# Last stage of a fused transformer kernel: softmax sums from ScalarE's accumulator, sums spread over heads by small tiles, SiLU through tanh, maxima in three parts

## The chip, the cores and the metric

The kernel runs on one core of one Trainium2 chip. The metric is the device time of one execution in microseconds (us). A core has five engines with queues of their own, which run in the order of the program and wait for each other through semaphores: TensorE (PE; its weight loads are PEld), VectorE (DVE), ScalarE (ACT), GpSimd (POOL) and SyncE (SP).

## The reference

Eight sequences of 256 tokens, 512 wide, go through four blocks, each added to the residual `x` with a gate:

```
x = x + tanh(g_xattn[0]) * L0_xattn(layernorm(x), ctx)      # causal attention, 16 heads of 32
x = x + tanh(g_ffn[0])   * L0_ffn(layernorm(x))             # ternary weights, silu(gate) * up, rms_norm
x = x + tanh(g_xattn[1]) * L1_xattn(layernorm(x), ctx)      # below
x = x + tanh(g_ffn[1])   * L1_ffn(layernorm(x))             # below

# L1_xattn: q, k after rms_norm with a weight; 16 heads of 32; 256 keys; not causal
scores = q k^T / sqrt(32); probs = softmax(scores); out = (probs v) o_w^T + o_b

# L1_ffn: weights ternary with one scale, activations rounded to 8 bits per token
gv = bitlinear(rms(x) * w_norm, w_gv)                       # 256x512 @ 512x4096
value, gate = split(gv); u = value * silu(gate)
out = x + bitlinear(u, w_out)                               # 256x2048 @ 2048x512
```

The change touches only the last two blocks, which the kernel runs as one stage, called the last stage below.

## The kernel before

Everything stays on the chip: `X` holds the residual of all sequences, `W1` the ternary weights of the last block, `ARENA` all other tiles of SBUF (so that the profile calls nearly every tile ARENA or W), `bank` the eight PSUM banks of 128 x 512 f32. The last stage is a hand-written software pipeline in turns. In turn t (3 to 7, the full turns) it does, for the sequence f = t: projections of queries and keys and their norms; for b = t-1: scores, maxima, probabilities and the weighing of the values; for c = t-2: the output projection and the inputs of the feed-forward; for d = t-3: the feed-forward. A turn for b = 7 (called turn 8) and a closing part follow. The order in each engine's queue is written out by hand, and each engine waits on semaphores.

Per sequence b the attention has these steps. There are 16 heads, in four groups g of four (one head j on each 32 partitions and on each bank 0 to 3).

- `c_scores(b, g)`, four times, spread over the first part of the turn: TensorE writes the scores of four heads, tokens on partitions, into banks 0 to 3 (L745); VectorE takes the maximum of each row (L1625). The banks are then free for the next group.
- `c_max_parts`, `c_max_turn`, `c_max_rows`: the negated maxima are split into two bf16 parts (L1633, L1635), turned so that tokens lie along the free dimension (L754), and copied to `MT` (L1640).
- `c_probs(b, g)`, four times in the second part of the turn: TensorE computes the scores again, with keys on partitions (L764), adds the negated maxima by a matmul with a selection matrix `selc` (L768), and ScalarE takes exp (L1178).
- `c_weigh(b, g)`: TensorE multiplies the values by the probabilities, and a matrix of ones by the same probabilities, which gives the sums of the softmax, repeated over the 32 rows of a head (both L783). VectorE takes the reciprocal of the sums (L1656) and multiplies (L1658).

The feed-forward of d has eight pieces j in a turn: `d_value_gate(d, j)` on TensorE writes a gate into one bank and a value into another (L795, 4 + 4 matmuls); ScalarE makes `silu(scale * gate)` (L1195, called `d_gate`), which frees the gate's bank; VectorE multiplies by the scaled value (L1725), and after each odd piece takes a maximum for the rounding (L1731). `d_scale_u` (L1737 to L1741) makes the scale, `d_round_u` (L1207) and `d_integers16` (L1750) round, `d_turn_u` transposes (L425, copied at L1002), and `d_out_product` (L825) is the last matmul.

Silu and Exp lie in different activation tables. `warm(...)` (L1182) is placed in ScalarE's queue where the table changes, twice a full turn.

Banks 4 to 7 are shared by all these results. A list gives the order of the tenants of each bank, and a tenant may be written when the one before it has raised its semaphore:

```
places.turn(turn, ("g0 v1 g3 pq0 v6 v7 ut0.0 y0 xt0", "v0 po1 v3 g4 v5 g7 tq1 w1 w2 w3", "po0 g2 kt0 v4 pq1 w0 qt1 ut1.1 y1",
                   "g1 v2 kt1 g5 g6 mt tq0 ut0.1 qt0 ut1.0 xt1"))
```

Here `g`, `v` are gate and value of a piece, `w` the weighed values, `po`, `pq` projections, `kt`, `tq`, `xt`, `ut`, `qt`, `mt` transposes, `y` the result. TensorE's order in the first part of a full turn is: scores 0, piece 0, po0, piece 1, scores 1, po1, pieces 2 and 3, scores 2, kt, pq0, pieces 4 and 5, scores 3, pq1, piece 6, mt, piece 7, and then the second part begins with probs 0.

## Time and profile before

| | us |
|---|---|
| median of 3 runs | 1142.21 (1140.67 to 1143.71) |
| the profiled execution | 1139.14 |
| its span in the trace | 1137.4 |
| full turns 3 to 7 (722.53 to 1025.42) | 302.9 |
| turn 8, first part (1025.42 to 1057.50) | 32.1 |

The page of the profile gives the busy time of each engine and the groups of instructions by line. Times in the rows are us from the start of the span. A timeline row gives start, duration, engine, line, operation, output<-input, count, and in brackets how long the engine sat idle before it and who released it. Successive rows of one engine can overlap, since the engine starts one instruction while the one before still drains: what an instruction costs in a row of such is the distance of the starts. TensorE runs an f32 matmul as two instructions, so that eight f32 matmuls stand as x16.

### The profile page before, as it was taken

Reading aid. Unit: us, or ns where it says so; the run is one execution under the profiler, and the core shown is the slowest. Engines: PE = TensorE matmul, PEld = TensorE weight load, DVE = VectorE, ACT = ScalarE, POOL = GpSimd, SP = SyncE. Lnnn points to the kernel's source line nnn. Section 1 sums busy time; section 2 is a strip of 40 time slices with the busy share of each in tenths; the row PEclk is TensorE's granted clock in tenths of the full one; section 3 lists DMA queues with packets and bytes.
Section 4 is the critical chain, followed back from the end, with each engine's and each line's share of the span. In section 5 each row is a group of like instructions: output and inputs, shape, how many; then the busy total and the mean of one; then the engine's idle time right before and its main releaser. Section 6 shows DMA issues by size and latency. Waiting matters only on the chain.

```text
span 1137.4 us, 25529 instructions
## 1 busy us (share of the span) xinstructions
PE 1096.0 (96%) x10342; PEld 669.3 (59%) x10450; DVE 832.7 (73%) x1440; ACT 567.2 (50%) x918; POOL 74.5 (7%) x180
## 2 busy tenths in 40 slices
PE   8899999999999999999999999899999999999998
PEld 3455555556777777777777655455454545454543
DVE  5688888788767648566565667886868778777795
ACT  3676667766433333333333452455554637372654
POOL 0000000000000000000001012010101010101010
PEclk9899999999999999999999999999999999999999
DMA  9565555443212011021010201101010100000001
GB/s 361 185 194 169 181 193 156 154 122 122 67 38 65 20 38 37 20 75 28 29 57 20 84 2 38 37 2 56 1 57 1 57 1 30 10 11 11 10 10 38
DMA packets 29268, 79.24 MB, mean 70 GB/s; under 512 B 3041, under 2 KB 3297, under 8 KB 28897
## 3 DMA queue, kind: packets, MB, share of 16 engines
q1 hardware_dynamic: 29152, 77.61, 21.0%
q8 instruction: 84, 1.38, 0.5%
q14 instruction: 32, 0.25, 0.1%
HBM read 65.02 MB, written 12.58 MB: 68 GB/s over the span
## 4 chain that ended last, share of the span: by engine, by line
PE 89%; issue 3%; ACT 3%; DVE 2%; DMA 2%; SPq 1%; POOL 0%; ACTq 0%; DVEq 0%; POOLq 0%
PE bank L587 10%; PE bank L586 10%; PE bank L692 10%; PE bank L672 9%; PE bank L545 9%; PE bank L795 8%; PE bank L425 5%; PE bank L825 5%; PE bank L783 5%; PE bank L745 3%; PE bank L764 3%; PE bank L477 2%; PE bank L498 2%; PE bank L510 2%; PE bank L450 2%
## 5 line engine op out<-in xcount | busy, mean ns | idle before, releaser
L586 PE MATMUL bank<-ARENA,W 128*128 128x256 f16 x1024 | 227.3, 273 | 0.7 <-issue 0.7
L587 PE MATMUL bank<-ARENA,W 128*128 128x256 f16 x1024 | 227.2, 273 | 0.0
L1002 ACT ACTIVATE ARENA<-bank 128x512 f32<-128x512 f32 (+3 forms) x143 | 92.9, 687 | 81.3 <-PE bank L425 32.6
L545 PE MATMUL bank<-ARENA 128*128 128x512 f32 x256 | 119.4, 609 | 1.4 <-DMA ARENA<-in_wkv 1.4
L795 PE MATMUL bank<-W,ARENA 128*128 128x512 bf16 x493 | 116.6, 382 | 2.5 <-issue 0.7
L692 PE MATMUL bank<-ARENA 128*128 128x512 f32 x256 | 116.9, 600 | 0.0
L672 PE MATMUL bank<-W,ARENA 128*128 128x512 bf16 x472 | 114.6, 379 | 2.2 <-issue 0.2
L586 PEld LDWEIGHTS bank<-ARENA,W 128*128 128x128 bf16 x1024 | 100.0, 98 | 19.5 <-issue 1.3
L587 PEld LDWEIGHTS bank<-ARENA,W 128*128 128x128 bf16 x1024 | 100.1, 98 | 17.9
L1002 ACT ACTIVATE ARENA<-ARENA 128x512 f16<-128x512 f32 x64 | 40.3, 630 | 136.1 <-DVE ARENA L1585 129.6
L1585 DVE SCALAR_TENSOR_TENSOR ARENA<-bank,ARENA 128x512 f32<-128x512 f32 x64 | 48.0, 750 | 76.4 <-PE bank L587 73.5
L1195 ACT ACTIVATE ARENA<-bank,ARENA 128x512 f32<-128x512 f32 x64 | 43.7, 685 | 112.7 <-PE bank L795 105.5
L1999 POOL TENSOR_TENSOR ARENA<-ARENA 128x2 f32<-128x2 f32 (+1 forms) x72 | 49.2, 684 | 673.0 <-DVE ARENA L1372 435.4
L795 PEld LDWEIGHTS bank<-W,ARENA 128*128 128x128 bf16 x512 | 49.0, 98 | 66.3 <-issue 11.6
L1116 ACT ACTIVATE ARENA<-bank 128x512 f32<-128x512 f32 x64 | 38.2, 596 | 91.5 <-PE bank L587 91.4
L1382 DVE TENSOR_REDUCE ARENA<-bank 128x4 f32<-128x512 f32 x64 | 58.3, 952 | 34.6 <-PE bank L450 34.4
L1625 DVE TENSOR_REDUCE ARENA<-bank 128x4 f32<-128x1024 f32 x64 | 75.2, 1218 | 9.3 <-PE bank L745 9.3
L545 PEld LDWEIGHTS bank<-ARENA 128*128 128x128 f32 x256 | 47.4, 192 | 56.4 <-issue 52.5
L672 PEld LDWEIGHTS bank<-W,ARENA 128*128 128x128 f16 x512 | 49.9, 99 | 48.8 <-issue 1.9
L1591 DVE TENSOR_TENSOR ARENA<-ARENA 128x512 f16<-128x512 f32 x64 | 44.2, 691 | 46.5 <-ACT ARENA L1002 46.5
L1656 DVE RECIPROCAL ARENA<-bank 128x256 f32<-128x256 f32 x32 | 56.2, 1756 | 29.6 <-PE bank L783 29.6
L692 PEld LDWEIGHTS bank<-ARENA 128*128 128x128 f32 x256 | 46.6, 190 | 52.6 <-issue 51.5
(179 smaller groups left out, 1766.5 us busy)
## 6 DMA issues: line engine op xcount, KB each, us to landing
W<-in_w SPq DMA_DIRECT2D x48, 512.0 KB, 4.0
ARENA<-in_w SPq DMA_DIRECT2D x24, 512.0 KB, 3.6
kv_store<-ARENA SPq DMA_DIRECT2D x32, 256.0 KB, 3.8
W<-kv_store SPq DMA_DIRECT2D x15, 512.0 KB, 4.0
ARENA<-in_ctxT SPq DMA_DIRECT2D x8, 512.0 KB, 3.8
X<-in_x SPq DMA_DIRECT2D x8, 512.0 KB, 5.8
ARENA<-in_ctx SPq DMA_DIRECT2D x8, 512.0 KB, 5.9
out<-X SPq DMA_DIRECT2D x16, 256.0 KB, 2.0
```

What stands on the lines that cost most here:

```text
L425: mm = pe.transpose(to[:, k * P:(k + 1) * P], tile, one)
L545: mm = pe.matmul(bank, bufA["KT"][:, b % 2 * KD + k, t * P:(t + 1) * P], W[:, k, :], start=(k == 0), stop=(k == KD - 1 and what == 1))
L586: pe.matmul(bank[:, i * S:(i + 1) * S], W0[:, at:at + P], xt_half(b, 0)[:, k, :], start=(k == 0), stop=False)
L587: mm = pe.matmul(bank[:, i * S:(i + 1) * S], W0[:, at:at + P], xt_half(b, 1)[:, k, :], start=False, stop=(k == KD - 1))
L672: mm = pe.matmul(banks[6 + t], hx(q, what)[:, i * S + t * P:i * S + (t + 1) * P], W0[:, UP_AT + m * D:UP_AT + (m + 1) * D], start=(m == 0 ...
L692: pe.matmul(to, src[:, k, t * P:(t + 1) * P], WQ[w][:, k, :], start=(k == 0), stop=False)
L783: mm = pe.matmul(part(to, j)[:, what * S:(what + 1) * S], lhs, bufC["PT"][:, h % 8, kb * S:(kb + 1) * S], start=(kb == 0), stop=True, skip ...
L795: mm = pe.matmul(to, QQ[d][:, t, k * P:(k + 1) * P], W1[:, at:at + D], start=(k == 0), stop=(k == KD - 1))
L825: mm = pe.matmul(to, UT[d, t][:, k * P:(k + 1) * P], W1[:, UP_AT + k * D:UP_AT + (k + 1) * D], start=(k == 0), stop=(k == KH - 1))
L1002: return act.activation(to, src, ACT.Copy)
L1382: got = v.tensor_reduce(NM[:, t, :, g % 2], bank[:, 0:4, t * P:t * P + (t + 1) * P], AX_X, ALU.max, negate=True)
L1625: got = v.tensor_reduce(NM[:, t, :, g], bank[:, 0:4, t * S:(t + 1) * S], AX_X, ALU.max, negate=True)
```

## The change

- For the sequences b = 2 to 6 (`summed_apart`), the ones-matmuls of `c_weigh` go (8 f32 matmuls for each of the four groups), and so does VectorE's reciprocal of each group. Instead, ScalarE takes exp of the first scores in place in PSUM, with the negated maximum as bias, and its accumulator gives the row sums: `c_sums`, 32 activations of 128 x 256 per sequence. The next group of scores may be written only after these are done (`s.c_se`).
- VectorE inverts the 32 sums per token, splits them into three bf16 parts (`c_sum_parts`), TensorE turns them (`rt`, 2 transposes), VectorE copies them (`c_sum_rows`), TensorE spreads them over the rows of the heads by 16 matmuls of 32 x 32 tiles into two banks (`rb0`, `rb1`), ScalarE copies these into `OT` (`c_spread_sums`), and VectorE multiplies.
- For d = 0 to 5 (`by_tanh`), silu(z) is computed as z/2 * (1 + tanh(z/2)): ScalarE takes tanh, VectorE makes `(tanh + 1) * gate` in an operation of its own (`s.d_gg`, which now frees the gate's bank), and then multiplies by the value. Tanh and Exp need no change of table here, so that the `warm` calls of the full turns go.
- The negated maxima are split into three bf16 parts in place of two.
- The factor of the scores moves from ScalarE's exp into the query's scale.
- VectorE's and ScalarE's orders are rearranged: in the first part of a turn the sums stand between the gates in ScalarE's queue.

```diff
         for turn in range(3, NB):
-            places.turn(turn, ("g0 v1 g3 pq0 v6 v7 ut0.0 y0 xt0", "v0 po1 v3 g4 v5 g7 tq1 w1 w2 w3", "po0 g2 kt0 v4 pq1 w0 qt1 ut1.1 y1",
-                               "g1 v2 kt1 g5 g6 mt tq0 ut0.1 qt0 ut1.0 xt1"))
+            places.turn(turn, ("g0 v1 g3 pq0 v6 v7 rb0 ut0.0 y0 xt0", "v0 po1 v3 g4 v5 g7 tq1 w1 w2 w3", "po0 g2 kt0 v4 pq1 rt w0 qt1 ut1.1 y1",
+                               "g1 v2 kt1 g5 g6 mt tq0 rb1 ut0.1 qt0 ut1.0 xt1"))
...
@@ tensor_program: c_scores
                     for j in range(4):
+                        if summed_apart(b) and g:
+                            pe.wait_ge(s.c_se, 32 * (b - FIRST) + 8 * (g - 1) + 2 * (j + 1))
...
+            def c_turn_sums(b):
+                to, sem, value = bank_c("rt", b)
+                pe.wait_ge(sem, value)
+                pe.wait_ge(s.c_rhl, b - FIRST + 1)
+                for t in range(TB):
+                    mm = pe.transpose(as16(to, BF16)[:, t * P:(t + 1) * P], bufC["RHL"][:, t, :], keep["identb"])
+                mm.then_inc(s.c_rt, 1)
+
+            def c_spread_sums(b):
+                for k in range(2):
...
+                    pe.wait_ge(s.c_rtr, b - FIRST + 1)
+                    for n in range(2):
+                        for j in range(4):
+                            mm = pe.matmul(part(to, j)[:, n * S:(n + 1) * S], part(keep["selc"], j)[:, 2 * k + n, 0:DH], part(bufC["RT"], j),
+                                           start=(n == 0), stop=True, skip_group_check=True)
+                    mm.then_inc(s.c_rb, 1)
...
@@ c_weigh
-                for what in range(2):
+                for what in range(1 if summed_apart(b) else 2):
...
@@ turns, TensorE
                 c_turn_q(f)
+                c_turn_sums(b)
                 c_probs(b, 1)
+                c_spread_sums(b)
                 c_weigh(b, 0)
...
@@ scalar_program
+            def c_sums(b, g, banks_of=(0, 1, 2, 3)):
+                for j in banks_of:
+                    for t in range(TB):
+                        h, scores = NG * j + g, banks[j][:, t * S:(t + 1) * S]
+                        act.wait_ge(s.c_rhl, b - FIRST)
+                        act.wait_ge(s.c_scr, 4 * b + g + 1)
+                        act.activation(scores, scores, ACT.Exp, bias=bufC["NM"][:, t, h:h + 1], accum_out=bufC["sums"][:, t, h:h + 1]
+                                       ).then_inc(s.c_se, 1)
...
             for turn in range(3, NB):
                 d_gate(d, 0)
+                c_sums(b, 0)
                 d_gate(d, 1)
                 c_square_k(f, 0)
                 c_square_k(f, 1)
                 d_residual(d, 0)
+                c_sums(b, 1, (0, 1))
+                d_gate(d, 2)
+                c_sums(b, 1, (2, 3))
+                d_gate(d, 3)
                 d_residual(d, 1)
-                d_gate(d, 2)
-                d_gate(d, 3)
                 c_turn_k(f)
+                c_sums(b, 2, (0, 1))
                 c_square_q(f, 0)
                 d_gate(d, 4)
+                c_sums(b, 2, (2, 3))
+                d_gate(d, 5)
                 both(d_round_u, d, 0)
-                d_gate(d, 5)
+                c_sums(b, 3, (0, 1))
                 c_square_q(f, 1)
                 d_gate(d, 6)
+                c_sums(b, 3, (2, 3))
                 d_gate(d, 7)
-                warm(ACT.Exp)
                 c_probs(b, 0)
                 c_turn_q(f)
                 c_probs(b, 1)
+                c_spread_sums(b)
                 both(d_turn_u, d, 0)
...
-                warm(ACT.Silu)
...
@@ vector_program: c_weigh
+                if summed_apart(b):
+                    v.wait_ge(s.c_rbr, 2 * (b - FIRST) + g // 2 + 1)
+                    v.tensor_tensor(bufC["OT"][:, g, :], to[:, 0:S], bufC["OT"][:, g, :], ALU.mult).then_inc(s.c_pvr, 1)
...
@@ d_value_gate
+                if by_tanh(d):
+                    v.scalar_tensor_tensor(out=gated, in0=gated, scalar=1.0, in1=bank_c(f"g{j}", d)[0], op0=ALU.add, op1=ALU.mult).then_inc(s.d_gg, 1)
+                    v.wait_ge(s.d_gg, 8 * d + j + 1)
...
@@ turns, VectorE
                 d_scale_u(d, 0)
-                d_weighted(c)
                 c_scores(b, 2)
                 d_value_gate(d, 4)
+                c_norm_q(f, 0)
                 d_value_gate(d, 5)
-                c_norm_q(f, 0)
                 c_scores(b, 3)
                 c_max_parts(b)
                 d_value_gate(d, 6)
                 c_max_rows(b)
-                d_integers16(d, 0)
                 c_norm_q(f, 1)
                 d_value_gate(d, 7)
+                c_sum_parts(b)
                 d_scale_u(d, 1)
+                c_sum_rows(b)
+                d_integers16(d, 0)
+                d_weighted(c)
+                c_weigh(b, 0)
                 d_peak(c)
                 d_inputs(c)
-                c_weigh(b, 0)
+                c_weigh(b, 1)
                 if f + 1 < NB:
                     stats(f + 1, s.c_ve)
-                c_weigh(b, 1)
```

`c_sum_parts` is a reciprocal of 128 x 32 and four more operations of that size, one after the other; `c_sum_rows` is one copy of 128 x 256 bf16.

## Rows read from the trace of the kernel before

**Rows 1.** The page: busy time, share of the span, instructions.

```profile
PE 1096.0 (96%) x10342; PEld 669.3 (59%) x10450; DVE 832.7 (73%) x1440; ACT 567.2 (50%) x918; POOL 74.5 (7%) x180
```

**Rows 2.** The chain of work that ended last, inside one full turn, by line.

```profile
by line: PE bank L692 23.5%; PE bank L795 23.3%; PE bank L783 12.5%; PE bank L825 11.3%; PE bank L425 7.9%; PE bank L745 7.2%; PE bank L764 7.1%; ACT ARENA L1002 1.7%; ACT ARENA L1178 1.7%; PE bank L768 1.6%; PE bank L694 1.1%; issue 1.0%; 
```

**Rows 3.** Windows: full turns, one turn's two parts, turn 8's first part.

```profile
core 0: us, PE busy (x) PEld busy (x) DVE busy (x) ACT busy (x) POOL busy (x), PEclk, DMA share, GB/s
722.53:1025.42 302.89, 294.86 (x2400) 153.60 (x2422) 236.55 (x399) 162.86 (x240) 30.92 (x89) 1.00 0.08 25
844.27:878.80 34.53, 34.37 (x173) 16.14 (x175) 26.85 (x41) 12.65 (x22) 5.62 (x17) 1.00 0.09 29
878.80:904.57 25.77, 24.79 (x312) 14.77 (x313) 20.64 (x41) 20.02 (x27) 0.70 (x1) 1.00 0.10 26
1025.42:1057.50 32.08, 29.55 (x198) 14.43 (x204) 26.89 (x44) 11.44 (x16) 3.27 (x11) 1.00 0.03 9
```

**Rows 4.** Timeline of TensorE in that turn.

```profile
852.56 1.15 PE L745 MATMUL bank<-W 32*128 32x256 f32 x16
...
876.86 0.28 PE L754 MATMUL bank<-ARENA 128*128 128x128 bf16 x2
...
878.80 1.15 PE L764 MATMUL bank<-W 32*128 32x256 f32 x16
879.77 0.40 PE L768 MATMUL bank<-ARENA 32*128 32x256 bf16 x8
...
884.43 1.05 PE L783 MATMUL bank<-ARENA 128*32 128x256 f32 x16
885.41 1.07 PE L425 MATMUL bank<-ARENA 128*128 128x128 bf16 x16
```

**Rows 5.** Timeline of VectorE in the same full turn.

```profile
854.64 2.35 DVE L1625 TENSOR_REDUCE ARENA<-bank 128x4 f32<-128x1024 f32 x2
...
860.04 1.27 DVE L1678 BATCH_NORM_STATS2 ARENA<-X 128x6 f32<-128x512 f32 x2
...
861.51 0.72 DVE L1725 SCALAR_TENSOR_TENSOR W<-bank,ARENA 128x512 f32<-128x512 f32 x1
862.27 1.22 DVE L1731 TENSOR_REDUCE ARENA<-W 128x1 f32<-128x1024 f32 x1
...
864.68 1.40 DVE L1691 SCALAR_TENSOR_TENSOR ARENA<-X,ARENA 128x512 f32<-128x512 f32 x2
...
876.38 0.19 DVE L1635 TENSOR_TENSOR ARENA<-ARENA 128x32 bf16<-128x32 f32 x1
...
886.84 1.75 DVE L1656 RECIPROCAL ARENA<-bank 128x256 f32<-128x256 f32 x1
```

**Rows 6.** Timeline of ScalarE in that turn.

```profile
851.89 0.69 ACT L1195 ACTIVATE ARENA<-bank,ARENA 128x512 f32<-128x512 f32 x1 [4.69 <-PE bank L795]
...
862.76 1.09 ACT L1002 ACTIVATE W<-bank 128x512 f32<-128x512 f32 x2 [1.82 <-PE bank L425]
...
878.83 1.28 ACT L1182 ACT_TABLE_LOAD   x1
...
882.10 1.57 ACT L1170 ACTIVATE W<-bank,ARENA 128x256 f32<-128x256 f32 x4
```

**Rows 7.** Groups by line and form, last stage: busy us, mean ns of one.

```profile
L1170 ACT ACTIVATE W<-bank,ARENA 128x256 f32<-128x256 f32 x20 | 7.9, 490 | 0.0
```

**Rows 8.** Timeline of ScalarE in the first stage: accumulator, 256-wide copy.

```profile
227.22 1.08 ACT L1055 ACTIVATE W<-W 128x1024 f32<-128x1024 f32 x1
228.17 0.22 ACT L1055 ACTIVATION_READ_ACCUMULATOR W<-W 128x1 f32 x1
228.26 0.61 ACT L1002 ACTIVATE ARENA<-bank 128x512 f32<-128x512 f32 x1
...
232.11 0.38 ACT L1002 ACTIVATE W<-bank 128x256 f32<-128x256 f32 x1 [1.81 <-PE bank L510]
232.39 1.05 ACT L1012 ACTIVATE W<-W 128x1024 bf16<-128x1024 f32 x1
```

More of the change, by code:

```diff
@@ L168, in build @@
         keep, kept = views(ARENA, KEEP)
+        keep["abs_sum"], keep["scl"] = keep["spare"][:, 0:24], keep["spare"][:, 24:48]
         rest = ARENA[:, (kept + 31) // 32 * 8:]
@@ L762, in c_probs @@
                     for j in range(4):
+                        if summed_apart(b) and g == 0:
+                            pe.wait_ge(s.c_se, 32 * (b - FIRST) + 24 + 2 * (j + 1))
                         pe.wait_ge(s.c_ex, 8 * b + max(0, 2 * (g - 1) + j // 2 + 1))
@@ L1194, in d_gate @@
                 act.wait_ge(s.d_g, 8 * d + j + 1)
-                act.activation(bufC["SG"][:, n % 2, :], bank_c(f"g{j}", d)[0], ACT.Silu, scale=keep["sv"][:, d % 2, t:t + 1]).then_inc(s.d_sg, 1)
+                act.activation(bufC["SG"][:, n % 2, :], bank_c(f"g{j}", d)[0], ACT.Tanh if by_tanh(d) else ACT.Silu,
+                               scale=keep["sv"][:, d % 2, t:t + 1]).then_inc(s.d_sg, 1)
             def d_turn_q(d):
```

98 lines of the change are left out of this document (72 added, 26 removed).

## The prediction

> **What bounds the kernel now.** I read the page first [rows 1]: TensorE is busy 96% of the span, VectorE 73%, ScalarE 50%. Then the chain of waits inside one full turn of the last stage [rows 2]: it runs over TensorE's lines, and ScalarE's hold 3.4%. The windows [rows 3] say the same: TensorE works 294.9 of 302.9 us in the five full turns, at the full clock. So today the stage is as long as TensorE's work, and work taken from TensorE is a gain, if the others still deliver in time. For that two parts of a turn must be kept apart, since the change adds in one and removes in the other [rows 3]. In the first (34.5 us, scores and feed-forward pieces) VectorE is busy 26.9 us and ScalarE 12.7; in the second (25.8 us, probabilities and weighing) 20.6 and 20.0. The reader is to see that VectorE has only 7.7 us left in the first part, and that all of the new exps and most new VectorE work go there. Times below are us from the start of a turn's first scores.
>
> **What the change removes.** The ones-matmuls of one group cost 0.98 us from their start to the next work [rows 4]: 4 groups x 5 sequences = 19.6 us of TensorE. Four reciprocals of 1.75 us a turn leave VectorE [rows 5], all in the second part. Two table loads of 1.28 us a turn leave ScalarE [rows 6]; the one shown ran under the matmuls of probs 0, the other at the end of a turn before ScalarE has work, so I take nothing for them.
>
> **What it adds to TensorE.** Two transposes, 0.3 us [rows 4], and 16 matmuls of 32 x 32 tiles. The nearest row has 8 of 32-row tiles with the same width in 0.40 us [rows 4]; I take 0.7 (bounds 0.6 and 0.8), and 1.0 in all a turn. Net TensorE work is 5 x (3.9 - 1.0) = 14.5 us less.
>
> **What one exp with a sum costs ScalarE.** No such row exists. A 256-wide activation with a pointer operand comes every (1.57 - 0.49) / 3 = 0.36 us (four in a row took 1.57 [rows 6], one alone lasts 0.49 [rows 7]), a plain one every 0.28 [rows 8]. Reading the accumulator delays the next start by 0.09 [rows 8] and itself lasts 0.22. So 0.45 us each, with bounds 0.37 (plain) and 0.7 (nothing overlaps: 0.49 + 0.22). That is 32 x 0.45 = 14.4 us a turn; ScalarE's first part grows from 12.7 to 27 us of busy time, which still fits 34.5. The load is not the problem, the order is.
>
> **What it adds to VectorE.** Eight `(tanh + 1) * gate` of 0.75 us a turn (L1725 is the same size [rows 5]), 7 of them before the second part; one waits for the other inside a piece. Parts and reciprocal of the sums are five operations of 0.19 to 0.22, 1.1 us, and the rows' copy 0.3. In a turn VectorE is about level (+6.0 +1.4 +0.4 for the third part of the maxima, -7.0), but the first part gets 5.7 us on 26.9 of 34.5.
>
> **Moved, at no cost.** The second residual goes from before piece 2 to behind tanh 3 on ScalarE; GpSimd's line of statistics waits for it and then ends near 23, and its readers come in the second part, near 50. `d_integers16` and `d_weighted` go from the first part of VectorE's queue to behind the sums; I count them there. The load and store queue waits for results (`d_res`), for turned keys (`c_kt`) and for weighed values (`c_pv`), all a turn or more ahead of need, and no transfer is added. The factor in the queries' scale changes no instruction's size; the earlier table load before turn 1 runs beside TensorE's work, and without that cover costs 1.3 us once.
>
> **The first part, by its chain.** Before, a next group of scores waited for VectorE's maxima alone, and a gate's bank for ScalarE alone. Now scores g+1 wait for maxima, then eight exps, and ScalarE's queue puts the tanh of the next pieces behind exps which wait for the maxima; VectorE's queue puts the next maxima behind those same pieces. The two in-order queues hand the work back and forth:
> - Maxima 0 end at 3.6; eight exps of 0.45 to 7.3. Tanh 1 ends at 8.4; VectorE's gate, value and reduce (0.78 + 0.78 + 1.13) to 11.1; maxima 1 (2.35 us [rows 5]) end at 13.4, some 0.7 later than before.
> - Four exps (1.8), tanh 2 (0.7), four exps, tanh 3: 18.4. VectorE meanwhile does piece 2 and the statistics (1.47) and is ready at 19.0. Gate and value of piece 3 1.55, reduce and scale 2.41 [rows 5], maxima 2: 25.3.
> - Four exps, a square (0.6), tanh 4, four exps, tanh 5: 30.9. Gate and value 5 with reduce 2.7, maxima 3: 36.0.
> - Four exps, square, tanh 6 (0.7): 39.1. Gate 6 (0.8) frees bank 7 for the turned maxima (`mt`), which stand ahead of piece 7 on TensorE: 40.0; then mt 0.3 and piece 7 1.75: probs 0 starts at 42.1.
>
> It started at 34.5. TensorE should idle in these places: 0.9 us at scores 2 (exps of group 1), 3.5 at value 5 (its bank 5 was gate 4's, now freed by VectorE), 3.1 at mt: 7.5 us.
>
> **The second part.** After probs 0 and the turned queries (44.4) TensorE waits for the parts of the sums, which VectorE makes after piece 7: 45.95, so 1.6 us of new wait. Probs 1, spreading, weighing 0: 49.3. The transposes of u need the banks `rb0`, `rb1`, freed by two ScalarE copies (L1002, some 0.5 us apart [rows 6]) that stand behind the exps of probs 1: 50.2 and 50.7. Then TensorE sets the pace again, less the ones-matmuls; the transposes of the next x wait some 0.5 us as now. The next turn starts at 67.0: 25.0 us against 25.8, of the 2.9 us of saved work only 0.8 come through.
>
> A turn is then 67.0 in place of 302.89 / 5 = 60.6 [rows 3]: 6.4 more, 32 over five turns.
>
> **Turn 8** has no exps for sums but still tanh with eight gate operations (6.0 us) on a VectorE busy 26.9 of 32.1 [rows 3]. By the same walk gate 5 waits for bank 6 (gate 4 by VectorE, 22.7 against 20.7), mt for bank 6 again (28.5 against 24.1), piece 7 for gate 6 (31.4), and probs 0 starts at 33.1 against 27.2. Little behind it gives that back; I take 5.5, with bounds 2 (gate 5's wait alone) and 6. The closing part keeps silu and its order.
>
> **Sum.** 32 + 5.5 = 37.5 us on the span of 1137.4, that is 1175; the execution itself took 1139.1, 1.7 more than its span, and the median of the runs is 3.1 above that. On the median: 1142.2 + 37.5 = 1180. With 0.37 us an exp the chain is 1.3 us a turn shorter (16 exps x 0.08): 1173. With 0.7 it is 4 to 5.5 us a turn longer (16 to 22 exps x 0.25): 1200 to 1207.
>
> **The rivals.**
> - *Cover holds, faster.* If VectorE and ScalarE keep up at each group of scores, only TensorE's work counts: 1142.2 - 14.5 = 1128. It decides at the distance of two groups of scores: before, 34.5 / 4 = 8.6 us; the loop of maxima, eight exps, two tanh, gate, value and reduce, needs 2.35 + 3.6 + 1.4 + 2.7 = 10 and more. It would need exps near 0.25 us. For it: the busy shares all fit. Against it: that distance. Chance 9%.
> - *Table loads on the path.* If the ten loads of 1.28 us held the exps of probs 0 and the first gates back, 13 us of the 37.5 come back: 1167. Against it: the one shown lies beside probs 0 on TensorE [rows 4, 6], and the other ends before any gate is ready. Chance 3%. The Trainium skill (ScalarE: Activation LUTs, "Table sets: the hidden batching unit") says to batch activations by set, with tanh and exp in one, and its page prices a switch at about 2.66 us with its drain; by that estimate ten switches saved are 27 us, and the time would be 1153. The trace shows 1.28 us for the load.
> - *Break-even.* A shorter loop, or a second part that gives back its whole 2.9 us a turn, and stalls of only that size: 1139 to 1146. Chance 4%.
> - *Half the stalls.* The walk counts an idle of TensorE where issue order leaves slack, or turn 8 costs 2: some 1150 to 1163. Chance 15%.
> - *Exps without overlap.* PSUM as both source and target, each read of the accumulator in full: 1200 to 1210, decided from 0.6 us an exp. Chance 12%.
>
> My forecast, 1163 to 1198, gets 57%.
>
> **How the numbers follow.** Slower is 57 + 15 + 12 + 3 = 87%, faster 9%, same 4% (0.3%, 3.4 us, is about what a measurement of this kernel can tell). For eight times in ten the range takes the forecast, the half of the stalls and the near end of the slow exps: 1153 to 1203.
>
> **What would show it.** Five turns of 66 to 68 us, with probs 0 some 42 us after scores 0. ScalarE: 160 exps with 160 accumulator reads, starts 0.45 us apart, in blocks of four whose idle before them ends on VectorE's maxima. TensorE: idle of about 3 us before value 5 and before mt, released by the new VectorE operation, 1.6 us before the turned sums. ScalarE still under 75% in a turn. The prediction is wrong if TensorE stays over 95% busy in the turns, or if the exps run closer than 0.3 us.

## The result, and the profile after

The changed kernel takes 1184.18 us (median of four runs, 1182.9 to 1184.4) against 1141.44 for the kernel before on the same chip: 1.0369 times as long, 95% interval 1.0354 to 1.0385. The forecast was 1180, with 1153 to 1203 as the range. The profiled execution took 1182.9 us, its span 1181.0.

Three lines of the page, after: busy time of each engine, the shares of the chain that ended last, and the new group of activations.

```profile
PE 1099.0 (93%) x10112; PEld 668.2 (57%) x10220; DVE 840.6 (71%) x1521; ACT 625.9 (53%) x1224; POOL 76.6 (6%) x180
...
PE 70%; DVE 11%; ACT 8%; issue 7%; DMA 2%; SPq 1%; POOL 0%; ACTq 0%; DVEq 0%; POOLq 0%
...
L1225 ACT ACTIVATE bank<-bank,ARENA 128x256 f32<-128x256 f32 x160 | 72.3, 461 | 58.6 <-DVE ARENA L1687 58.6
```

VectorE and ScalarE are busy 71% and 53% of the span [rows 1 for before]. TensorE has 10112 instructions where it had 10342 (its busy time is no smaller, since part of them ran at a lower clock, as shown below), and still the kernel is 43 us longer. The last row says where to look: before the exps ScalarE sat idle for 58.6 us, all of it ended by VectorE's maxima (L1687), and the chain has 19% on these two engines. That this idle time also costs time is read from the timelines below.

The windows, after: five full turns, turn 8 up to its probs 0, and the rest; then the two parts of the third full turn [rows 3 for before]. Columns: stretch, length, busy time with counts, TensorE's granted clock, DMA share, GB/s.

```profile
core 0: us, PE busy (x) PEld busy (x) DVE busy (x) ACT busy (x) POOL busy (x), PEclk, DMA share, GB/s
724.01:792.40 68.39, 60.82 (x438) 31.08 (x441) 49.13 (x96) 44.88 (x110) 6.82 (x18) 0.94 0.08 25
792.40:859.44 67.04, 57.03 (x436) 29.51 (x441) 47.70 (x94) 44.99 (x110) 6.81 (x18) 1.00 0.08 25
859.44:926.53 67.09, 58.63 (x437) 30.17 (x441) 47.69 (x94) 44.99 (x110) 6.82 (x18) 0.97 0.08 26
926.53:994.27 67.74, 60.14 (x437) 30.86 (x441) 47.69 (x94) 44.99 (x110) 6.82 (x18) 0.95 0.08 23
994.27:1061.31 67.04, 58.31 (x428) 29.71 (x432) 45.35 (x87) 43.99 (x108) 5.66 (x17) 0.97 0.03 12
1061.31:1095.99 34.68, 27.52 (x146) 12.45 (x148) 28.61 (x44) 6.90 (x10) 3.29 (x11) 0.91 0.02 8
1095.99:1181.00 85.01, 77.76 (x572) 40.22 (x578) 62.94 (x121) 46.88 (x56) 4.19 (x11) 0.98 0.06 20
859.44:901.30 41.86, 37.07 (x172) 17.23 (x174) 30.39 (x47) 26.99 (x86) 5.65 (x17) 0.96 0.07 25
901.30:926.53 25.23, 21.55 (x266) 12.94 (x267) 17.30 (x47) 18.00 (x25) 1.17 (x1) 1.00 0.09 29
```

A full turn has 67.04 us at the full clock; at a granted clock of 0.94 or 0.95 it has 68.39 and 67.74. Its first part has 41.86 against 34.5, its second 25.2 against 25.8. The span is 43.6 us longer, made up so: 1.5 ahead of the turns (they start at 724.01 in place of 722.53), 337.3 - 302.9 = 34.4 in the full turns, 34.68 - 27.16 = 7.5 in turn 8 before its probs 0 (which before ran from 1025.42 to 1052.58), 0.2 in the rest.

TensorE's timeline of the third full turn, after (scores 2, 3, the waits, probs 0 and the turned sums; the turn starts at 859.44) [rows 4 for before]:

```profile
859.44 1.15 PE L761 MATMUL bank<-W 32*128 32x256 f32 x16
...
876.10 1.00 PE L761 MATMUL bank<-W 32*128 32x256 f32 x6
877.32 1.13 PE L761 MATMUL bank<-W 32*128 32x256 f32 x10 [0.22 <-ACT bank L1225]
878.37 1.09 PE L439 MATMUL bank<-ARENA,W 128*128 128x128 f32 x8
...
888.68 1.89 PE L832 MATMUL bank<-W,ARENA 128*128 128x512 bf16 x4 [2.98 <-DVE ARENA L1818]
890.50 1.85 PE L761 MATMUL bank<-W 32*128 32x256 f32 x16
892.28 3.70 PE L706 MATMUL bank<-ARENA 128*128 128x512 f32 x8
...
899.36 0.28 PE L770 MATMUL bank<-ARENA 128*128 128x128 bf16 x2 [1.44 <-DVE ARENA L1818]
...
901.30 1.15 PE L782 MATMUL bank<-W 32*128 32x256 f32 x16
...
905.44 0.27 PE L796 MATMUL bank<-ARENA 128*128 128x128 bf16 x2 [1.75 <-DVE ARENA L1704]
...
907.02 0.62 PE L806 MATMUL bank<-ARENA 32*32 32x256 bf16 x16
```

Scores 2 wait for the exps of group 1. From their start to that of the next work it is 2.27 us (876.10 to 878.37), where scores 0 take 1.08, so the wait is 1.2 us; the bracket shows 0.22 of it, and the rest lies between the matmuls of the first row. The three longer waits are those of the forecast too: value 5 waits for gate 4's bank, mt for gate 6's, both now freed by VectorE's new operation (L1818), and the turned sums wait for their parts (L1704). The idle at mt seems to be half of the 3.1 us said. But from the start of the four value matmuls to that of scores 3 it is 1.82 us (0.97 one turn earlier), and from there to the next start 1.78 (1.08 for scores 0): the granted clock was low. The windows of that stretch, and the same two waits one turn earlier, where the clock stayed at 1.00:

```profile
888.68:892.28 3.60, 3.60 (x20) 1.65 (x21) 3.27 (x5) 3.60 (x8) 0.00 (x0) 0.54 0.00 0
```

```profile
821.65 1.04 PE L832 MATMUL bank<-W,ARENA 128*128 128x512 bf16 x4 [2.98 <-DVE ARENA L1818]
822.62 1.18 PE L761 MATMUL bank<-W 32*128 32x256 f32 x16
...
832.33 0.28 PE L770 MATMUL bank<-ARENA 128*128 128x128 bf16 x2 [2.96 <-DVE ARENA L1818]
```

At the full clock the idle at mt is 2.96. In the third full turn 1.5 us of it went into slower matmuls, and mt started at the same distance (39.92 and 39.93 us), since it waits for VectorE and not for them.

VectorE's timeline of the same turn, after [rows 5 for before]: maxima 2, gate 4, value 4, maxima 3, gate 6.

```profile
882.30 2.35 DVE L1687 TENSOR_REDUCE ARENA<-bank 128x4 f32<-128x1024 f32 x2
887.94 0.69 DVE L1818 SCALAR_TENSOR_TENSOR ARENA<-ARENA,bank 128x512 f32<-128x512 f32 x1 [3.29 <-ACT ARENA L1249]
888.66 0.75 DVE L1821 SCALAR_TENSOR_TENSOR W<-bank,ARENA 128x512 f32<-128x512 f32 x1
...
892.98 2.35 DVE L1687 TENSOR_REDUCE ARENA<-bank 128x4 f32<-128x1024 f32 x2
...
898.62 0.69 DVE L1818 SCALAR_TENSOR_TENSOR ARENA<-ARENA,bank 128x512 f32<-128x512 f32 x1 [2.40 <-ACT ARENA L1249]
```

ScalarE's timeline of the same turn, after [rows 6 for before]: the first exps of group 0, then the first of group 2, tanh 4 and the first of group 3.

```profile
863.21 0.45 ACT L1225 ACTIVATE bank<-bank,ARENA 128x256 f32<-128x256 f32 x1 [0.85 <-DVE ARENA L1687]
863.58 0.19 ACT L1225 ACTIVATION_READ_ACCUMULATOR bank<-bank,ARENA 128x1 f32 x1
863.67 0.44 ACT L1225 ACTIVATE bank<-bank,ARENA 128x256 f32<-128x256 f32 x1
...
884.74 0.45 ACT L1225 ACTIVATE bank<-bank,ARENA 128x256 f32<-128x256 f32 x1 [4.53 <-DVE ARENA L1687]
...
887.12 0.71 ACT L1249 ACTIVATE ARENA<-bank,ARENA 128x512 f32<-128x512 f32 x1
...
895.42 0.45 ACT L1225 ACTIVATE bank<-bank,ARENA 128x256 f32<-128x256 f32 x1 [3.12 <-DVE ARENA L1687]
```

Read the two together and the loop is there. VectorE's maxima 2 run to 884.65; ScalarE, idle for 4.53 us, begins its exps at 884.74 and gets to tanh 4 at 887.12; VectorE, idle for 3.29 us, begins gate 4 at 887.94 and gets to maxima 3 at 892.98. Each engine is idle while the other works, so that their times add up.

### The profile page after: what moved, and what is told of

It reads as the page before. It is cut to its first block, busy times and chain, and to the rows that moved or that the text cites. A ratio compares the mean times of both kernels' runs of the same rounds, so it can differ in the third digit from the quotient of the medians.

```text
span 1181.0 us, 25759 instructions
## 1 busy us (share of the span) xinstructions
PE 1099.0 (93%) x10112; PEld 668.2 (57%) x10220; DVE 840.6 (71%) x1521; ACT 625.9 (53%) x1224; POOL 76.6 (6%) x180
## 4 chain that ended last, share of the span: by engine, by line
PE 70%; DVE 11%; ACT 8%; issue 7%; DMA 2%; SPq 1%; POOL 0%; ACTq 0%; DVEq 0%; POOLq 0%
PE bank L600 9%; PE bank L601 9%; PE bank L686 9%; PE bank L559 9%; PE bank L862 5%; DVE ARENA L1687 5%; PE bank L439 4%; ACT bank L1225 3%; PE bank L820 3%; PE bank L832 3%; PE bank L706 3%; PE bank L782 2%; DVE ARENA L1818 2%; PE bank L491 2%; PE bank L512 2%
## 5 line engine op out<-in xcount | busy, mean ns | idle before, releaser
L1041 ACT ACTIVATE ARENA<-bank 128x512 f32<-128x512 f32 (+3 forms) x153 | 98.5, 685 | 72.7 <-PE bank L439 24.1
L1225 ACT ACTIVATE bank<-bank,ARENA 128x256 f32<-128x256 f32 x160 | 72.3, 461 | 58.6 <-DVE ARENA L1687 58.6
L1441 DVE TENSOR_REDUCE ARENA<-bank 128x4 f32<-128x512 f32 x64 | 58.3, 953 | 34.4 <-PE bank L464 34.2
L1687 DVE TENSOR_REDUCE ARENA<-bank 128x4 f32<-128x1024 f32 x64 | 75.2, 1218 | 9.5 <-PE bank L761 9.5
L1217 ACT ACTIVATE ARENA<-bank 128x1024 f32<-128x1024 f32 x64 | 62.1, 1024 | 33.3 <-PE bank L786 33.3
```

The source lines that it names most:

```text
L1041: return act.activation(to, src, ACT.Copy)
L1217: act.activation(bufC["PT"][:, h % 8:h % 8 + 2, :], bank[:, j:j + 2, :], ACT.Exp).then_inc(s.c_ex, 1)
L1225: act.activation(scores, scores, ACT.Exp, bias=bufC["NM"][:, t, h:h + 1], accum_out=bufC["sums"][:, t, h:h + 1]).then_inc(s.c_se, 1)
L1441: got = v.tensor_reduce(NM[:, t, :, g % 2], bank[:, 0:4, t * P:t * P + (t + 1) * P], AX_X, ALU.max, negate=True)
L1687: got = v.tensor_reduce(NM[:, t, :, g], bank[:, 0:4, t * S:(t + 1) * S], AX_X, ALU.max, negate=True)
```

## The experiments

All times in us are medians over the runs of a kernel; the kernel before had 1141.53 us beside the first four kernels, 1140.57 beside the next four and 1140.45 beside the last two. "Turn" is the median of the five full turns in the profiled execution, "probs 0" the median of its start after the turn's first scores, and the last column the same distance in turn 8. These three come from one execution each (that of e5 took 1147.96 us, 4.6 more than its median), and a lower granted clock in some turn is part of them.

| kernel | us | ratio to before [95%] | turn | probs 0 | turn 8, probs 0 |
|---|---|---|---|---|---|
| before | 1141.44 | 1 | 60.6 | 34.8 | 27.2 |
| after | 1184.18 | 1.0369 [1.0354, 1.0385] | 67.1 | 41.9 | 34.7 |
| e1_tanh_alone | 1160.18 | 1.0163 [1.0142, 1.0184] | 63.4 | 35.6 | 34.6 |
| e2_sums_alone | 1154.86 | 1.0118 [1.0092, 1.0144] | 63.4 | 38.5 | 27.6 |
| e3_maxima_first | 1150.50 | 1.0087 [1.0059, 1.0115] | 61.1 | 35.9 | 33.0 |
| e4_half_the_exps | 1172.24 | 1.0268 [1.0248, 1.0289] | 65.9 | 40.4 | 34.4 |
| e5_turn8_by_silu | 1143.39 | 1.0031 [1.0016, 1.0046] | 61.4 | 35.9 | 27.6 |
| e6_waits_taken_out | 1139.87 | 0.9996 [0.9984, 1.0008] | 60.4 | 36.2 | 27.6 |
| e7_before_without_loads | 1139.49 | 0.9996 [0.9987, 1.0006] | 60.3 | 34.5 | 27.2 |
| e8_late_release | 1165.98 | 1.0225 [1.0210, 1.0240] | 65.0 | 40.5 | 31.8 |
| e9_banks_swapped | 1132.91 | 0.9940 [0.9923, 0.9957] | 59.2 | 34.9 | 27.6 |
| e10_spread_first | 1132.61 | 0.9936 [0.9920, 0.9953] | 59.0 | 34.9 | 27.6 |

The theory of the forecast (the loop): ScalarE's exps stand behind VectorE's maxima, the maxima behind the pieces, the pieces behind a tanh that stands behind the exps. Its rivals: the load itself (so much more work for ScalarE and VectorE), and a single part of the change that costs all of it.

### The two halves of the change, each alone

`e1_tanh_alone` takes the sums away again; the tanh, its operation on VectorE and the three maxima parts stay (TensorE's turning and spreading of the sums and their banks go with them; those lines are cut below).

```diff
         def summed_apart(b):
-            return FIRST <= b < NB - 1
+            return False
@@ ScalarE's and VectorE's order of a full turn
-                c_sums(b, 0)
...
-                c_sum_parts(b)
-                c_sum_rows(b)
```

> The changed kernel without the sums on ScalarE: the ones-matmuls and reciprocals are back, the exps for sums and the spreading are gone; tanh, its VectorE operation and the orders stay. Theory (two in-order queues hand the work back and forth): without exps between the tanh of the pieces, a full turn should be only 1 to 2 us longer than before, so 61.5 to 62.5 us, probs 0 about 35.5 us after scores 0; turn 8 is as in the changed kernel, 7.5 us longer. In all 1157 us (1150 to 1163). Rival (the tanh form itself is the price, by VectorE's eight more operations a turn): VectorE is at 53 of 61 us, and most of the 43 us stay: 1175 or more. Rival (the exps' load on ScalarE is the whole price): 1142.

`e2_sums_alone` keeps the sums and takes VectorE's new operation away; the factor that it computed is left out, and the gate's bank is again free when ScalarE has read it.

```diff
         def by_tanh(d):
-            return d < NB - 2
+            return False
...
-            raised[f"g{j}"], raised[f"v{j}"] = (s.d_gg, 8, j, 3), (s.d_u, 8, j, 3)
+            raised[f"g{j}"], raised[f"v{j}"] = (s.d_sg, 8, j, 3), (s.d_u, 8, j, 3)
@@ d_gate
-                act.activation(bufC["SG"][:, n % 2, :], bank_c(f"g{j}", d)[0], ACT.Tanh if by_tanh(d) else ACT.Silu,
+                act.activation(bufC["SG"][:, n % 2, :], bank_c(f"g{j}", d)[0], ACT.Tanh if d < NB - 2 else ACT.Silu,
```

> The changed kernel with the sums, but the gate is ScalarE's tanh(scale * gate) alone for d = 0 to 5: the factor (1 + tanh) * gate is left out, so VectorE has no new operation in a piece and the gate's bank is freed by ScalarE. Theory: each of pieces 1, 3, 5 and 6 shortens the chain of a turn by 0.78 us; probs 0 comes about 38.7 us after scores 0 in place of 41.9, a turn is about 64 us, and turn 8 is as before the change. 1184 - 5 x 3 - 7.5 = 1161 us (1155 to 1167). Rival (the exps' load is the whole price): unchanged in the full turns, 1176. Rival (the late release of the gates' banks is the whole price): back to 1145 or less.

Measured: 1160.2 and 1154.9. In e1 probs 0 came at 35.56, as expected, but the second part took 27.3 to 29 us in four of the five turns, and a turn 63.4 where 61.5 to 62.5 was expected: with the ones-matmuls back, TensorE waits 1.40 us for VectorE's reciprocal and multiplication before weigh 3, and in two of these turns the granted clock of this part was 0.94. In e2 probs 0 came at 38.53 (expected 38.7), and the whole kernel was 6 us quicker than the 1161 expected, just outside the range. Taking away the sums gives back 24 us of 43, taking away the operation for tanh, with the later release of the bank, 29: together more than there is. So the cost is not a sum of two prices: each half costs more beside the other, which fits the loop and does not prove it. e3, the smallest edit, says more.

### The order alone

`e3_maxima_first` does all the work of the changed kernel, on the same engines. Only VectorE's order differs: of pieces 1, 3 and 5 it makes the gate first, then the maxima, and the multiplication by the value with its reduce behind them.

```diff
-                d_value_gate(d, 1)
+                d_value_gate(d, 1, "g")
                 c_scores(b, 1)
+                d_value_gate(d, 1, "v")
...
-                d_value_gate(d, 3)
-                d_scale_u(d, 0)
+                d_value_gate(d, 3, "g")
                 c_scores(b, 2)
+                d_value_gate(d, 3, "v")
+                d_scale_u(d, 0)
...
-                d_value_gate(d, 5)
+                d_value_gate(d, 5, "g")
                 c_scores(b, 3)
                 c_max_parts(b)
+                d_value_gate(d, 5, "v")
```

> The changed kernel with nothing left out; only VectorE's order in a full turn changes: of pieces 1, 3 and 5 only the gate operation stands ahead of the next maxima, the value and its reduce (and the scale after piece 3) follow behind the maxima. Theory: the exps of the next group begin 1.5, 3.3 and 3 us earlier, and probs 0 comes about 37 us after scores 0 in place of 41.9: 5 us a turn, 1184 - 25 = 1159 us (1153 to 1166). Rival (load of ScalarE or VectorE, or contention in PSUM): the work is the same, so the time stays within 3 us of 1184.

Measured: 1150.5, 34 us less than after, and better than the expected range of 1153 to 1166; probs 0 at 35.93, where 37 was expected. e3's VectorE timeline around maxima 2 (its turn starts at 846.15), and below it the windows of that turn's two parts and of turn 8's first:

```profile
864.24 0.65 DVE L1819 SCALAR_TENSOR_TENSOR ARENA<-ARENA,bank 128x512 f32<-128x512 f32 x1
864.81 2.35 DVE L1687 TENSOR_REDUCE ARENA<-bank 128x4 f32<-128x1024 f32 x2
867.08 0.74 DVE L1824 SCALAR_TENSOR_TENSOR W<-bank,ARENA 128x512 f32<-128x512 f32 x1
```

```profile
846.15:882.08 35.93, 34.97 (x176) 16.32 (x175) 30.22 (x47) 27.25 (x86) 5.64 (x17) 1.00 0.08 29
882.08:907.25 25.17, 21.80 (x268) 12.85 (x267) 17.29 (x47) 18.00 (x25) 1.16 (x1) 1.00 0.09 30
1030.30:1063.30 33.00, 28.12 (x149) 12.53 (x149) 27.92 (x43) 6.89 (x10) 3.28 (x11) 0.95 0.02 9
```

Maxima 2 start 864.81 - 846.15 = 18.7 us into the turn, in the changed kernel 882.30 - 859.44 = 22.9. VectorE's 30.2 us and ScalarE's 27.3 in the first part are the same as after (30.4 and 27.0), and the part is 5.9 us shorter. So the load did not hold the turn up; the order did. Moving three multiplications of 0.75 us, each with its reduce of 1.22 behind it, and after piece 3 the scale, was worth 30.5 us over the five full turns, about 6 a turn. (Of the 33.1 us between the two profiled executions 1.7 more lie in turn 8, whose order is the same in both; they go with the clock, see the end.) The load rival is out. The second part has not moved (25.17 against 25.23), as it should not.

### The size of an exp

`e4_half_the_exps` makes one exp of 128 x 512 for each head in place of two of 128 x 256, so that the maximum of the other tokens is used for half of them and the sums of a head run together; the number of exps in the loop is halved.

```diff
-                    for t in range(TB):
-                        h, scores = NG * j + g, banks[j][:, t * S:(t + 1) * S]
...
-                        act.activation(scores, scores, ACT.Exp, bias=bufC["NM"][:, t, h:h + 1], accum_out=bufC["sums"][:, t, h:h + 1]
-                                       ).then_inc(s.c_se, 1)
+                    h = NG * j + g
+                    act.activation(banks[j], banks[j], ACT.Exp, bias=bufC["NM"][:, 0, h:h + 1], accum_out=bufC["sums"][:, 0, h:h + 1]
+                                   ).then_inc(s.c_se, 2)
```

> The changed kernel with one exp of 128 x 512 for each bank in place of two of 128 x 256, with the maximum of the first token block for both and one sum in place of two: 80 exps instead of 160, the sums of the first block then cover both and those of the second are left at 1. A bank costs 0.60 us of ScalarE in place of 0.90. Theory: only the exps on the chain count, 0.6 us for each block of four, in four blocks of a turn: 2.4 us a turn, 1172 us (1168 to 1176). Rival (ScalarE's load is the price): 16 x 0.3 = 4.8 us a turn, 1160. Rival (the count of small instructions doesn't matter at all, the tanh form does): 1184.

Measured: 1172.24. The wide exps start 0.66 us apart where two narrow ones need 0.90, so each pair is 0.24 us shorter. The full turns of the profiled execution are 1.5 us shorter than after on average (337.3 - 329.6, by five), the medians of the runs differ by 2.4 a turn (1184.18 - 1172.24, by five): 6 to 10 pairs of the 16 in a turn. The walk had 8 pairs on the path. So part of ScalarE's exps set the end, and not all.

### Turn 8

`e5_turn8_by_silu` is e3 with silu in the pieces of turn 8, which has no exps for sums and so no reason to stay in the table with Exp; it costs two table loads, and the gates' banks of turn 8 are freed by ScalarE again.

```diff
         def by_tanh(d):
-            return d < NB - 2
+            return d < NB - 3
...
+        raised.update({f"g{j}": (s.d_sg, 8, j, 3) for j in range(8)})
...
+                else:
+                    warm(ACT.Silu)
...
+            warm(ACT.Exp)
             c_probs(b, 0)
```

> The kernel with the maxima ahead (nothing left out), and in turn 8 the gates (d = 5) through silu as before the change, with a table load at either end of the turn, the gates' banks freed by ScalarE. Theory: probs 0 of turn 8 comes 27 to 28 us after scores 0 in place of 33.0 and nothing else changes, so 1150.5 - 5.5 = 1145 us (1142 to 1148). Rival (table loads cost what they last): two loads of 1.28 us take back half of it, 1148 or more.

Measured: 1143.4, 7 us less than e3, of which turn 8 gives 5.4: it reaches probs 0 after 27.64 us in place of 33.00. So all but 0.5 us of the loss of turn 8 came with the tanh form: VectorE's extra operation, and the gates' banks that are freed behind it. e8 below tells these two apart. The two table loads cost nothing that shows: e2, which has none in turn 8, reaches probs 0 there after 27.63 us. Of the changed kernel's 34.68 us the walk's 33.1 is what e3 shows (33.00, granted clock 0.95), and the rest goes with the clock (see the end).

### The waits that were left

`e6_waits_taken_out` is e5 with mt in another bank and ahead of piece 6, and the parts of the sums ahead of piece 7.

```diff
-            places.turn(turn, ("g0 v1 g3 pq0 v6 v7 rb0 ut0.0 y0 xt0", "v0 po1 v3 g4 v5 g7 tq1 w1 w2 w3", "po0 g2 kt0 v4 pq1 rt w0 qt1 ut1.1 y1",
-                               "g1 v2 kt1 g5 g6 mt tq0 rb1 ut0.1 qt0 ut1.0 xt1"))
+            places.turn(turn, ("g0 v1 g3 pq0 v6 v7 rb0 ut0.0 y0 xt0", "v0 po1 v3 g4 v5 mt g7 tq1 w1 w2 w3", "po0 g2 kt0 v4 pq1 rt w0 qt1 ut1.1 y1",
+                               "g1 v2 kt1 g5 g6 tq0 rb1 ut0.1 qt0 ut1.0 xt1"))
@@ TensorE
-                d_value_gate(d, 6)
                 c_max_turn(b)
+                d_value_gate(d, 6)
@@ VectorE
-                d_value_gate(d, 6)
                 c_max_rows(b)
+                d_value_gate(d, 6)
                 c_norm_q(f, 1)
-                d_value_gate(d, 7)
                 c_sum_parts(b)
+                d_value_gate(d, 7)
```

> As the run with silu in turn 8, and two waits taken out of the full turns: the turned maxima (mt) get bank 5 and stand ahead of piece 6 on TensorE, so that they no longer wait for gate 6; the parts of the sums are made ahead of piece 7 on VectorE, so that the turned sums wait less. Nothing is left out. The two waits are 0.96 and 1.75 us a turn in the run with the maxima ahead. Theory: a full turn is then 58.6 to 59.5 us in place of 61.1, against 60.6 before the change: 1145 - 10 = 1135 us (1131 to 1140), faster than before. Rival (VectorE's total work, 47.5 us plus its dead time between short operations, is the floor of the turn): no gain over the run with silu in turn 8.

Measured: 1139.87, no more than level with before, where 1135 was expected. The two waits of e3 (0.96 us at mt, 1.75 at the turned sums) are gone, but smaller ones stand in their place. e6's TensorE timeline, mt, the last value matmuls of piece 7, and the transposes of u:

```profile
876.83 0.28 PE L771 MATMUL bank<-ARENA 128*128 128x128 bf16 x2 [0.33 <-DVE W L1828]
...
880.43 1.04 PE L833 MATMUL bank<-W,ARENA 128*128 128x512 bf16 x4 [0.72 <-DVE W L1828]
...
888.73 1.11 PE L440 MATMUL bank<-ARENA 128*128 128x128 bf16 x16 [0.69 <-ACT ARENA L1042]
```

Mt and value 7 wait for a multiplication by the value, whose bank they inherit. A turn gained 0.7 us at the full clock (60.39 for e3's 61.10), not the 2.7 of the two waits, since the next late thing stood close behind.

`e9_banks_swapped` gives mt, value 7 and the turned queries other banks, and moves one reduce of VectorE behind the maxima's rows.

```diff
-            places.turn(turn, ("g0 v1 g3 pq0 v6 v7 rb0 ut0.0 y0 xt0", "v0 po1 v3 g4 v5 mt g7 tq1 w1 w2 w3", "po0 g2 kt0 v4 pq1 rt w0 qt1 ut1.1 y1",
-                               "g1 v2 kt1 g5 g6 tq0 rb1 ut0.1 qt0 ut1.0 xt1"))
+            places.turn(turn, ("g0 v1 g3 pq0 mt v6 tq0 rb0 ut0.0 y0 xt0", "v0 po1 v3 g4 v5 g7 tq1 w1 w2 w3", "po0 g2 kt0 v4 pq1 rt w0 qt1 ut1.1 y1",
+                               "g1 v2 kt1 g5 g6 v7 rb1 ut0.1 qt0 ut1.0 xt1"))
@@ VectorE
                 c_max_rows(b)
+                d_value_gate(d, 5, "r")
                 d_value_gate(d, 6)
```

> As the run with the waits taken out, nothing left out. Its full turns are 60.4 us and still idle 0.33 us before the turned maxima (value 5 frees their bank) and 0.72 before value 7 (value 6 frees its bank), and about 0.6 us before probs 0. Here the turned maxima get bank 4 ahead of value 6, value 7 goes to bank 7 behind gate 6, the turned queries to bank 4, and VectorE copies the maxima ahead of piece 5's reduce. Theory: these waits go, a turn is 59.0 to 59.6 us, 1139.9 - 5 = 1135 us (1132 to 1138). Rival (VectorE's and ScalarE's own work now sets the pace, and a wait taken out comes back in the next place): within 0.5 us a turn of 60.4, 1138 to 1141.

Measured: 1132.91, the first kernel that beats the one before: 0.9940 [0.9923, 0.9957]. Its five full turns (723.86 to 1019.36) take 295.5 us, with TensorE busy 286.3 of them, where before took 302.9 [rows 3]. The longest wait that is left in the second part (the spreading waits for the copy of the turned sums):

```profile
883.30 0.62 PE L807 MATMUL bank<-ARENA 32*32 32x256 bf16 x16 [0.99 <-DVE ARENA L1721]
```

`e10_spread_first` aimed at that wait: the copy of the turned sums stands ahead of the last reduce on VectorE (not shown below), and the spreading ahead of probs 1 on TensorE and ScalarE.

```diff
                 c_turn_sums(b)
-                c_probs(b, 1)
                 c_spread_sums(b)
+                c_probs(b, 1)
```

> As the run with the banks swapped, and the spreading of the sums stands ahead of probs 1 on TensorE and ScalarE, the copy of the turned sums ahead of piece 7's reduce on VectorE. Nothing is left out. It should fill the time in which probs 1 waits for the exps of probs 0 (0.6 us) and take out the wait of 0.69 us for ScalarE's copies ahead of the transposes of u, but ScalarE's exps of probs 1 begin 1.1 us later. Theory: 0.3 to 1 us a turn less than the run with the banks swapped, 1132 us (1129 to 1136). Rival (the later exps hold probs 2 back): no gain or 0.5 us a turn more.

Measured: 1132.61, 0.3 us under e9, which can't be told from nothing. The wait was not taken out but exchanged: in e10's third full turn TensorE idles 1.21 us before the spreading, until ScalarE has copied the turned queries (L1210), whose bank 4 the first spread sums inherit.

### Table loads, and late release of a bank

`e7_before_without_loads` is the kernel before with Tanh where it had Silu in the full turns and turn 8, without the multiplication that tanh needs, and without 12 table loads. These are the loads that the change takes away (the forecast counted the ten of the full turns).

```diff
-                act.activation(bufC["SG"][:, n % 2, :], bank_c(f"g{j}", d)[0], ACT.Silu, scale=keep["sv"][:, d % 2, t:t + 1]).then_inc(s.d_sg, 1)
+                act.activation(bufC["SG"][:, n % 2, :], bank_c(f"g{j}", d)[0], ACT.Tanh if d < NB - 2 else ACT.Silu, scale=keep["sv"][:, d % 2, t:t + 1]).then_inc(s.d_sg, 1)
...
-                warm(ACT.Exp)
                 c_probs(b, 0)
```

> The kernel before, with silu(scale * gate) replaced by tanh(scale * gate) for d = 0 to 5 (the gate's factor is left out) and the table loads of turns 3 to 8 taken away, nothing else. It tells what twelve table loads of 1.28 us are worth. Theory (they lie where ScalarE waits or beside TensorE's work): 1141.5 us, no change beyond 0.3%. Rival (they are on the path): 13 to 27 us faster.

Measured: 1139.49, ratio 0.9996 [0.9987, 1.0006]. Two groups by line, the first of before and the second of e7, count the loads that `warm` made:

```profile
L1182 ACT ACT_TABLE_LOAD x15 | 19.2, 1283 | 0.3
```

```profile
L1182 ACT ACT_TABLE_LOAD x3 | 3.8, 1283 | 0.1
```

Twelve loads of 1.28 us are worth at most 1.5 us (the interval's lower end), and the best guess is 0.5. This rival has fallen. The Trainium skill (ScalarE: Activation LUTs, "Table sets: the hidden batching unit") has the switch as the thing to batch away; in this kernel it was not on the path, so there was next to nothing to win.

`e8_late_release` is e2 with one thing changed: the gate's bank counts as free when VectorE has multiplied by the value, not when ScalarE has read it.

```diff
-            raised[f"g{j}"], raised[f"v{j}"] = (s.d_sg, 8, j, 3), (s.d_u, 8, j, 3)
+            raised[f"g{j}"], raised[f"v{j}"] = (s.d_u, 8, j, 3), (s.d_u, 8, j, 3)
```

> As the run with the sums alone (the gate is ScalarE's tanh alone, the factor (1 + tanh) * gate is left out for d = 0 to 5, no new VectorE operation in a piece), but a gate's bank is freed by VectorE's multiplication with the value in place of ScalarE. It tells the operation's time from the late release of the bank. Theory (the loop sets the pace, the banks' waits only show it): full turns at most 0.5 us longer than the 63.35 of that run; in turn 8, where no exps stand in the loop, the release itself is the wait, and probs 0 comes 30 to 32 us after scores 0 in place of 27.6. 1155 + 5 = 1160 us (1157 to 1163). Rival (the release is what costs in all turns): near the changed kernel's 1184.

Measured: 1165.98, 11 us over e2 (8.7 between the spans of the profiled executions), more than expected. Turn 8 lost 4.2 (27.6 to 31.8), as expected. Of the full turns, two ran at the full clock in both kernels and lost 0.6 us each (63.91 for 63.36, 63.23 for 62.68), close to the 0.5 that was thought. Two more lost 2.2 at a granted clock of 0.97, and the first one took 65.0 in place of 66.4, which in e2 had a clock of 0.95. TensorE's timeline, value 5 and mt, first of e2 and then of e8:

```profile
879.92 1.04 PE L832 MATMUL bank<-W,ARENA 128*128 128x512 bf16 x4 [1.01 <-ACT ARENA L1249]
...
889.87 0.29 PE L770 MATMUL bank<-ARENA 128*128 128x128 bf16 x2 [1.43 <-ACT ARENA L1249]
```

```profile
881.76 1.04 PE L832 MATMUL bank<-W,ARENA 128*128 128x512 bf16 x4 [1.85 <-DVE W L1821]
...
891.71 0.29 PE L770 MATMUL bank<-ARENA 128*128 128x128 bf16 x2 [2.26 <-DVE W L1821]
```

The same two places wait, 0.8 us longer each, but value 5 starts 27.5 us into the turn in place of 26.6 and mt 37.4 in place of 36.6: 0.85 later in all and not 1.7, since what e8 waits more before value 5, e2 waits at scores 3 just behind it (880.89 to 882.80 for 1.07 us of matmuls). No work was added: only who frees the bank. In a full turn at the full clock the release so costs 0.6 us, and from e8's 63.91 to the 67.04 of the changed kernel it is 3.1 more, for VectorE's extra operation. In turn 8 the two are about equal: of the 4.2 us some 1.6 are the low clock of the last matmuls before probs 0 (see the end), which leaves 2.6 for the release by this estimate, and from there to e3's 33.0 it is 2.8 for the operation.

## Why the prediction was right, step by step

**The forecast and its cause held.** 1184.2 against 1180, and the cause is shown: order alone, with the same work, gives 34 of the 43 us back, 30.5 of them in the full turns whose order it changes (e3), a shorter exp shortens the turn by fewer pairs than there are (e4), and late release of a bank has its own price (e8). Part of the closeness is luck. On the span the sum was 37.5 us and the change cost 43.6. The 6 us that it lacked are 2.3 in the full turns, 2.0 in turn 8, 1.5 ahead of the turns and 0.2 in the rest. The forecast came out nearer because it added 4.8 us from the span to the median of the runs, where the runs after have 3.2.

- *An exp with its sum every 0.45 us:* right. Starts at 863.21 and 863.67; the read lies under the next exp. The rival of exps without overlap fell with that row. With 0.66 for the double width (e4), 256 more elements cost 0.21, and 0.24 of the 0.45 doesn't depend on the width.
- *The first part:* walked to 42.1, measured 41.9. Exps 0 started at 3.8 (3.6) and were done by 7.6 (7.3), maxima 2 ended at 25.2 (25.3), maxima 3 at 35.9 (36.0), mt began at 39.9 (40.0).
- *Where TensorE idles:* 2.98 before value 5 for 3.5, 2.96 before mt for 3.1 where the clock stayed full. At scores 2 it is 1.2 for 0.9 (2.27 for 1.08 us from their start to the next; the bracket of the row shows only 0.22). Together 7.1 for 7.5.
- *The second part:* 25.2 against 25.0, with 1.75 at the turned sums for 1.6.
- *A turn:* 67.04 at the full clock against 67.0.
- *Turn 8* is the term that was mis-sized: 5.5 forecast, 7.5 measured. The walk itself gave 5.9 (33.1 against 27.2), and e3, with the same order in turn 8, has it (33.00); the changed kernel has 1.7 us more. The lower clock behind the idle times was not in the sum.
- *Ahead of the turns* 1.5 us that the sum did not have. It is no work of the change: TensorE idles 2.79 us there in both kernels, and what follows up to the first scores takes 4.18 us at a granted clock of 0.68 (after) and 2.87 at 1.00 (before). e7 leaves out only a table load there, and yet its turns start at 723.74: 4.36 us behind the same idle of 2.79. In e10 they start at 722.70.
- *The full turns* cost 34.4, not 32: 1.4 and 0.7 us of the difference lie in the first and the fourth, with a granted clock of 0.94 and 0.95. Some 0.4 of the first turn's is there at the full clock too (e3 has 61.52 for 61.10).

**The rivals.** "Cover holds, faster" was wrong for this kernel and half right for a sibling: with other orders and banks in the full turns, and silu again in turn 8, the kernel runs in 1132.9 (e9), 7.5 us under the 1140.5 of before beside it, where TensorE's saved work alone allows 14.5. Its stated condition, exps near 0.25 us, was too strict: exps stayed at 0.45. "Half the stalls" and "break-even" describe the times of e3 and e6, not the change as made. "Table loads on the path" fell with e7.

What stays open: how the 7 us by which e9 and e10 stay above what the saved work alone allows divide (TensorE idles 1.8 us in e9's third full turn, 0.99 of it before the spreading, and e10, which aimed at that wait, put one of 1.21 in its place), what the third part of the maxima costs by itself, since no run takes it out alone, and why the clock fell after one idle and not after an equal one.

## What to carry to other kernels

When work moves from a busy engine to two idle ones, don't ask whether their busy shares leave room; write down who waits for whom, in queue order, from one hand-over to the next, and compare that loop's length with the distance at which the first engine comes back for the result. If the loop is longer, look first for what stands in a queue inside the loop without belonging to it, and for who frees each buffer: here three multiplications with their reduces, put behind the maxima, gave back 34 of the 43 us with no work removed. Silu in the one turn without sums gave 7 more, and two further changes of order and banks 3.5 and 7 (from e5 to e6 and from e6 to e9). Look for a table switch on the path before paying to avoid it.
